# A decoder on one core: 64-row scores and an identity product ahead of each head's scores in layer 1's shared attention

## The reference

```python
x = _layernorm(x + _L0_attn_ref(x, ...))
x = _layernorm(x + _L0_xattn_ref(x, mask, ctx, ...))
x = _layernorm(x + _L0_ffn_ref(x, ...))
x = _layernorm(x + _L1_attn_ref(x, ...))
x = _layernorm(x + _L1_xattn_ref(x, ctx, ...))     # the stage of this change
x = _layernorm(x + _L1_ffn_ref(x, ...))
```

```python
q = (x @ Wq + bq).reshape(1, B * N, H, hd)
kv = (cond @ Wkv + bkv).reshape(1, -1, 2, H, hd)
q = _fq_sym(q * scale, axis=-1); k = _fq_sym(k, axis=-1); v = _fq_sym(v, axis=2)
attn = softmax(einsum('bhqd,bhkd->bhqk', q, k))
attn = _fq_unsigned(attn, axis=-1)
out = einsum('bhqk,bhkd->bhqd', attn, v) @ Wp + bp
```

## Time and profile before

| | |
|---|---|
| median of three runs | 1417.89 us |
| the profiled execution's own time | 1417.26 us |
| its span | 1415.5 us |
| mean granted TensorE clock over the span | 0.907 |
| PE busy | 1237.8 us, 87% |
| DVE busy | 1046.5 us, 74% |
| ACT busy | 675.3 us, 48% |
| POOL busy | 135.1 us, 10% |

### The profile page before, as it was taken

How to read it: one execution, slowest core, us unless ns; L and a number is a source line. 1 busy time by engine, 2 the same in 40 slices (tenths; PEclk the granted TensorE clock), 3 DMA queues, 4 the chain that set the end, 5 groups by cost and what they waited for, 6 DMA issues and landing times.

```text
span 1415.5 us, 24455 instructions
## 1 busy us (share of the span) xinstructions
PE 1237.8 (87%) x9108; PEld 850.1 (60%) x9113; DVE 1046.5 (74%) x2349; ACT 675.3 (48%) x1286; POOL 135.1 (10%) x223
## 2 busy tenths in 40 slices
PE   6979999999999999999899999989899746677686
PEld 3747666766766766766676676656777623333344
DVE  6778578588677767858857775744888788889877
ACT  2336435434533633643553363442444358878751
POOL 2210010010011001002001100000000011111101
PEclk9989999999999999999999999999999955555588
DMA  7331002000100200200010013000300179989910
GB/s 240 154 105 63 12 12 66 13 1 16 63 12 16 62 12 12 66 12 5 26 49 12 12 63 120 20 23 24 78 8 9 31 124 167 173 151 181 166 23 30
DMA packets 176117, 86.06 MB, mean 61 GB/s; under 512 B 138240, under 2 KB 170368, under 8 KB 175744
## 3 DMA queue, kind: packets, MB, share of 16 engines
q1 hardware_dynamic: 174848, 84.13, 25.3%
q10 hardware_dynamic: 1152, 0.36, 0.1%
HBM read 43.57 MB, written 5.24 MB: 34 GB/s over the span
## 4 chain that ended last, share of the span: by engine, by line
PE 63%; DVE 19%; ACT 6%; issue 6%; DMA 5%; POOL 1%; SPq 0%; DVEq 0%; POOLq 0%; ACTq 0%
PE ps_t L1890 12%; PE ps_p L1874 11%; PE ps_s L2123 8%; PE ps_o L2040 5%; DMA w_moe<-w_moe 4%; PE ps_o L2030 4%; PE ps_o L1955 4%; PE ps_o L2123 3%; PE ps_p L1932 3%; DVE probs L1275 2%; ACT w_moe L1116 2%; PE ps_s L1932 2%; PE ps_o L1959 2%; DVE w_moe L1778 2%; DVE row_max L1281 1%
## 5 line engine op out<-in xcount | busy, mean ns | idle before, releaser
L1890 PE MATMUL ps_t<-ident,probs 128*128 128x128 f32 x1072 | 170.3, 280 | 28.5 <-ACT probs L1065 8.0
L925 ACT ACTIVATE probs<-probs 128x512 f32<-128x512 f32 x184 | 115.6, 628 | 136.6 <-DVE probs L1275 136.6
L1890 PEld LDWEIGHTS ps_t<-ident,probs 128*128 128x128 f32 x1072 | 123.2, 142 | 78.1 <-issue 37.9
L887 ACT ACTIVATE probsT<-ps_t 128x512 f32<-128x512 f32 x232 | 136.5, 589 | 64.0 <-PE ps_t L1890 63.8
L2123 PE MATMUL ps_s<-w_moe,xbT 128*128 128x352 f32 x352 | 122.1, 471 | 0.0
L1874 PE MATMUL ps_p<-w_qkv,xinT 128*128 128x512 f32 (+1 forms) x240 | 104.8, 560 | 11.4 <-DMA xinT<-in_xT 7.6
L2399 PEld LDWEIGHTS ps_p<-vals,w_moe 128*128 128x128 f16 x1024 | 37.2, 105 | 97.7 <-DMA w_moe<-w_moe 76.4
L831 POOL TENSOR_TENSOR rms<-mean_sq,neg_half 128x8 f32<-128x8 f32 x40 | 67.1, 1679 | 267.3 <-DVE mean_sq L1309 267.3
L887 ACT ACTIVATE bigT<-ps_t 128x512 f32<-128x512 f32 (+1 forms) x128 | 69.0, 553 | 33.3 <-PE ps_t L1890 31.4
L2399 PE MATMUL ps_p<-vals,w_moe 128*128 128x16 f16 x1024 | 48.2, 176 | 38.6 <-DMA w_moe<-w_moe 37.9
L2123 PEld LDWEIGHTS ps_s<-w_moe,xbT 128*128 128x128 f32 x352 | 64.0, 194 | 22.1 <-issue 1.5
(11 more groups left out here) (342 smaller groups left out, 2736.5 us busy)
## 6 DMA issues: line engine op xcount, KB each, us to landing
w_out<-in_wT_out SPq DMA_DIRECT2D x8, 2048.0 KB, 8.4
w_moe<-in_wT_gu SPq DMA_DIRECT2D x1, 5632.0 KB, 17.6
w_moe<-in_wT_down SPq DMA_DIRECT2D x1, 2816.0 KB, 10.2
keys<-keys2T SPq DMA_DIRECT2D x8, 256.0 KB, 2.0
keys2T<-keys SPq DMA_DIRECT2D x4, 512.0 KB, 10.4
w_moe<-w_moe SPq DMA_TRANSPOSE x128, 3.3
w_qkv<-in_wT_qkv SPq DMA_DIRECT2D x3, 512.0 KB, 4.9
w_qkv<-in_wT_qkv SPq DMA_DIRECT2D x1, 1536.0 KB, 8.3
```

The source lines that it names most:

```text
L887: nc.scalar.activation(dst, src.bitcast(BF16) if dst.dtype == BF16 else src, ACT.Copy)\
L925: nc.scalar.activation(probs[:, at % 4, :], probs[:, at % 4, :], ACT.Exp).then_inc(L0.exped, 1)
L1890: ins = nc.tensor.transpose(dst[:, i * P:(i + 1) * P], src(i), ident_b[:] if bf else ident[:])
```

## The change

Each product of the scores takes all 64 rows of its half, in place of 48. And ahead of each head's pair of scores, behind the wait for the bank, PE issues one identity product of 512 columns into the first bank of the pair. The scores overwrite it (`start=True`).

```diff
--- before.py
+++ after.py
@@ -2380,8 +2380,11 @@
                         turned("qs", LAST)
                     if u >= 3:
                         pe.wait_ge(exp2, u - 2)
+
+
+                    dense(psum[:, 0, :], 1)
                     for n in range(2):
-                        r = slice(STK * n, STK * n + 3 * HD1)
+                        r = slice(STK * n, STK * n + STK)
                         ins = nc.tensor.matmul(psum[:, n, :], (own if h % 2 == n else other)[r, h // 2, :],
                                                keys2T[r, h % 2, :, h // 2, :], start=True, stop=True)
                     ins.then_inc(s2, 1)
```

## The result

The median of the changed kernel is 1422.01 us (eight runs, 1419.02 to 1422.9), beside 1417.81 us for the kernel before on the same chip: ratio 1.0027, 95% interval 1.0017 to 1.0037. So it is slower, by 4.2 us. The forecast was 1418.5 us, +0.6; the time lies inside the range, but on the side to which I had given 0.34. The clock did become mixed, though its mean over 1150:1345, 0.59, lies just under the 0.6 to 0.8 that I had named as the sign. Two sizes were off, and the product costs about what the rule that I had set aside would make it cost.

A forecast was written before the change was run, and what follows sets the result against it. In layer 1's shared attention no engine was full and DMA nearly: SP's queue, 1.38 us a head, plus gaps. Out_project -1.5, ring +1.7 and DMA hiccups +0.4 made +0.6 us on 1417.89: 1418.5 us, range 1411 to 1425.

The forecast's parts named there:

- the rule that I had set aside: A weight load overlaps products in flight only on other row groups; the identity product would cost 0.1 us more where exposed.
- Step (1): Score products on 64 rows instead of 48: time is set by the 512 columns, so the rows cost nothing.
- Step (2): Identity product ahead of each head's scores: adds 0.43 us at 1.2 GHz; at 2.4 GHz the sum is zero.
- Step (3): At 1.2 GHz, the ring of three score banks at heads 1 to 8 loses 0.3 us a tile; total with head 13 +5.1.
- Step (3) at head 13: At 1.2 GHz, head 13's scores follow out_project, nothing else is late and SP idles: +0.43 us.
- Step (4): At 2.4 GHz, out_project ahead of head 13 gets 0.86 us shorter, seven times: -6.0 us.
- Step (5): Clock in layer 1's shared attention: rises around head 9 to 13, falls again, half speed in most of heads 1 to 8.
- products beside DMA hiccups: Products standing late beside DMA hiccups, a tenth of one product each by choice: +0.4 us.
- B: Rival: clock stays at 1.2 GHz; loss at head 13's scores and the ring, 1423.0 us (+5.1), bound +9.0; chance 0.30.
- the mixed case: Clock rises and falls in each tile, out_project at 2.4 GHz in two to five of seven; range 1414.5 to 1422 us.
- A: Rival: the clock is released for good, out_project faster in all seven tiles, 1411.9 us (-6.0); chance 0.25.
- C: Rival: nothing shows, SP's queue covers all or the clock changes where only DVE is late; 1418; chance 0.45 with the forecast.

The follow-up runs named there:

- e1_rows64: The changed kernel without the identity product, so the 64 rows alone: 1418.18 us beside 1417.43 for the kernel before, ratio 1.0002.
- e2_32rows: The changed kernel with its added product on 32 of the 128 rows, still 512 columns: 1427.39 us beside 1417.43 for the kernel before, ratio 1.0075.
- e3_two: The changed kernel with two identity products in place of one ahead of each head's scores: 1417.91 us beside 1417.43 for the kernel before, ratio 1.0006.
- e12_change: The changed kernel, unaltered, run again on another chip: 1420.95 us beside 1418.69 for the kernel before, ratio 1.0019.

## Why the prediction was right in kind and wrong in size

**Step (1), 64 rows: right for the time, not for the clock.** e1_rows64 costs +0.75 us within an interval that holds zero. But the rows have an effect that I didn't think of: in the profiles 0.54 beside 0.50 alone, and 0.59 beside 0.54 with the product. By the medians it is worth some 2 us there (+6.2 against +4.2 over the kernel before, on two chips, with intervals that overlap).

**Step (2), "it adds 0.43 us to each head's way", and at 2.4 GHz "the sum is zero": too small.** The prediction says that it would be wrong "if the product cost more than its 512 columns", and it does. The product costs 0.539 us at 1.2 GHz and 0.31 at 2.4. At full clock that is 0.31 - 0.22 = +0.09 in place of zero. My evidence against the rule of "TensorE: Matmul & The Clock Gate" of the Trainium skill, Part 3, was products that follow one another on all rows, where no time for a load shows. Here scores on half the array follow a product on all rows, which is another case, and about 0.1 us shows, as much as that rule would leave. That it is the load is my reading; the spacing alone is shown.

The trace of before had this case, in layer 0: products of the identity on all rows, followed by products on 64 rows.

```profile
221.05 0.63 PE L1919 MATMUL ps_p<-mask_window,ident_b 128*128 128x512 bf16 x1
221.62 0.59 PE L1932 MATMUL ps_p<-w_out 64*128 64x128 f32 x2
...
229.84 0.38 PE L1919 MATMUL ps_p<-mask_window,ident_b 128*128 128x512 bf16 x1
230.15 0.38 PE L1932 MATMUL ps_p<-w_out 64*128 64x128 f32 x2
```

From one start to the next it is 0.564 us at 1.2 GHz (three such pairs) and 0.309 at 2.4 (29 pairs). So the size could have been read before the change: a product's cost is to be looked up where it has the same neighbours.

**Step (3), the ring: the mechanism was right, the size was not.** The step reads "between nothing and 0.86 a tile I take 0.3". Measured with the clock held down by e2_32rows: 0.79 us a tile for heads 0 to 12, 0.50 of it at head 8. I had taken one round of the ring, 1.39 us a head with the product, as leaving "no slack", and then let each head's slack absorb first. With the measured 0.54 the round is (3.74 + 0.54)/3 = 1.43 us, slower than the queue's 1.38. What I didn't ask is what the slack was for. It covered most of DVE's 1.1 us at head 8: before the change the lead is 1.13 us at head 7 and 0.15 at head 8, and the gap between is 1.48, 0.10 over the queue's 1.38. The earlier trace rows shows the ring at head 1 and tells nothing of that; a look at the heads around DVE's other work would have.

**Step (3) at head 13: 0.69, not 0.43.** e2_32rows again. There the exponentials of heads 12 and 13 stand 3.34 us apart in place of 3.03, and the lead at head 12, taken as the table takes it at head 7, is 0.14 us in place of 0.53. So 0.3 us is a longer way, and 0.39 is the lost lead once more: "nothing else is late" overlooked that SP's queue was late at head 12.

**Step (4), the price of a fast out_project: right.** I had 0.86 us. From out_project's start to the next product on PE it takes 1.85 us at 1.2 GHz and 0.95 at 2.4 in the changed kernel; with nothing ahead of the scores 1.98 and 1.04. That streaming halves and the rest stays was a sound estimate. The 0.88 by which head 13's gap fell in e3_two is no second measurement of it, since two products stand in that gap.

**Step (5), the clock: mixed, but not at the right place.** I expected it to rise around heads 9 to 13, with "half of" out_projects at 2.4 GHz. In the changed kernel five of seven take 1.75 to 1.85 us to the next product, and two 0.95. Tile 3 is one of the five:

```profile
1239.67 2.05 PE L2342 MATMUL ps_p<-w_qkv,attT 128*128 128x256 f32 x4
...
1241.51 0.63 PE L1899 MATMUL ps_o<-ident_b 128*128 128x512 bf16 x1
...
1242.08 0.60 PE L2388 MATMUL ps_o<-keys2T,w_qkv 64*128 64x512 bf16 x1
...
1244.13 0.38 PE L1899 MATMUL ps_s<-ident_b 128*128 128x512 bf16 x1
...
1244.44 0.39 PE L2388 MATMUL ps_s<-keys2T,w_qkv 64*128 64x512 bf16 x1
```

The clock rises behind out_project, near 1244, where only DVE is late: there it is worth nothing. It rises behind out_project's start in all five, 3.5 to 4.3 us behind it in three. In the other two, tiles 4 and 6, it is 1.8 and 2.1 us: out_project itself is still slow, but head 13's product and scores are faster, and from out_project's start to head 13's exponential it takes 4.2 and 4.35 us in place of 4.7. In the two tiles with a fast out_project the clock rose only 0.3 and 0.4 us before it. So the number of fast ones in a profile is in part luck; e12_change, the same kernel, has three.

**The sum.** Forecast: -1.5 for out_project, +1.7 for the ring, +0.4 for the rest, +0.6. By the table, times seven: head 13 -0.8, head 8 +3.7, heads 9 to 12 +1.05, heads 0 to 7 +0.3, and the first tile is 0.7 us shorter (22.27 to 21.60): +3.5. So head 13 gave half of out_project's term, the ring took three times its own, and the 0.4 for products beside DMA hiccups has no row of its own. The profiled 4.4 and the medians' 4.2 have the stage's later start in them, +0.84 in these two profiles, which I can't lay to the change: across the fourteen kernels here, all the same up to that point, the first issue falls between 1145.7 and 1150.1 us.

**Luck.** The time lies inside the range because the range was drawn around all of B as well; the mixed case's own range ended at 1422. With the clock held down the product costs 10 us (e2_32rows), where my sum of step (3) had 5.1. That the change stayed near +4 is owed to head 13, which is 0.81 us a tile shorter than in e2_32rows though only two of seven out_projects are fast.

**The rivals.** B, at full strength, is e2_32rows, and would have been worth 10 us, beyond the +9.0 that I had called its bound. A's clock is e3_two's, and it didn't bring its 6 us, since two products ahead of the scores eat them. With the products behind the scores most of A's gain did come: -4.7 and -4.2 us against the kernel before on the same chip, of the -6.0 that I had priced. C fell: the change's interval, 1.0017 to 1.0037, doesn't hold 1.

## What to carry to other kernels

Work that is there only to keep TensorE's clock up belongs where PE waits for what isn't late for anyone, here ahead of its wait for the DMA and behind the scores; the table of waits names that place. Ahead of an operation that another engine waits for, it is paid each time, and here that came to as much as the clock gave back (two products) or more (one). And before slack is counted as free, look for the work that it covers once in each tile: a lead that is 1.1 us at head 7 is spent at head 8.

## What was not expected of the hardware

- With 512 columns streamed either way, the added product on 32 rows left the clock at 0.50 with PE busy for 185 of 195 us; on 128 rows it was 0.59 and 0.61 with 174 and 173 us, and two of them 0.96 with 160 us.
- Scores on 64 rows in place of 48, the added rows all zero on the keys' side, took the clock from 0.50 to 0.54 alone and from 0.54 to 0.59 with the product (one profile of each, and of e1_rows64 the one with the highest clock; the change again 0.61). The mean clocks over the program of the other executions go the same way.
- A product on all rows followed by products on half the array holds PE for 0.539 us at 1.2 GHz and 0.31 at 2.4, where products on all rows follow one another in 0.43 and 0.22. In layer 0 of the kernel before it is 0.56 and 0.31 ahead of products on 64 rows.
- Behind the same half-busy stretch of gate and up (PE busy for 1.98 of 4 us) the clock fell in e3_two and e1_rows64 and held in the changed kernel. Such a fall costs 1.5 us (12 products in 4.07 us in place of 2.60) and is a part of what one profile differs from another by.
